# A four-layer graph and attention network on one core: residual sums, clamps, division and stores rearranged, with 20 unread matmuls on TensorE

## The reference, cut to what matters

```
x = x + y @ wo.T                                  # y: attention, softmax over keys, 4 heads
flat  = rmsnorm(x, ln2_w)
probs = softmax(flat @ router_w.T); tp, ti = top_k(probs, 2); tp = tp / (sum(tp) + 1e-9)
for e in range(8):
    hh  = silu(flat @ w1[e].T) * (flat @ w3[e].T)  # 341 hidden units
    out = out + weights[:, e] * (hh @ w2[e].T)
return x + out
```

## Time and profile before

| what | value |
|---|---|
| median of 3 runs | 590.49 us (589.0 to 591.74) |
| the profiled execution, its own time | 591.75 us |
| its span, first to last instruction | 590.0 us, mean granted clock 0.928 |
| TensorE busy | 493.3 us (84%) |
| VectorE busy | 435.3 us (74%) |
| ScalarE busy | 319.3 us (54%) |
| GpSimd busy | 265.2 us (45%) |
| DMA | 91.66 MB, mean 155 GB/s |

### The profile page before, as it was taken

One profiled execution on the slowest core, in us unless ns is written; L12 is line 12 of the kernel. 1 busy time (PEld: TensorE's weight loads), 2 busy tenths in 40 slices (PEclk: granted clock), 3 DMA queues, 4 the chain that ended last, 5 costly groups with the idle time before them and its releaser, 6 DMA issues.

```text
span 590.0 us, 11473 instructions
## 1 busy us (share of the span) xinstructions
PE 493.3 (84%) x3865; PEld 279.4 (47%) x3865; DVE 435.3 (74%) x1075; ACT 319.3 (54%) x533; POOL 265.2 (45%) x289
## 2 busy tenths in 40 slices
PE   2999994879999799998676788899899967878870
PEld 1534333567777645553332243232353246778860
DVE  6898947788999955647779498699977217848854
ACT  0787886867999500111143454476367626656750
POOL 3000003423455320200426589599827644868872
PEclk9999996999999989999868878999999968989995
DMA  8999973200008660011204341000112753869975
GB/s 302 398 423 422 420 257 107 90 20 16 24 18 347 253 143 14 0 41 40 70 3 134 106 127 50 30 2 1 65 49 74 248 189 95 269 215 388 339 261 162
DMA packets 39570, 91.66 MB, mean 155 GB/s; under 512 B 7488, under 2 KB 24944, under 8 KB 35168
## 3 DMA queue, kind: packets, MB, share of 16 engines
q1 hardware_dynamic: 35792, 86.11, 41.7%
q0 software_dynamic: 2272, 4.69, 2.2%
q10 hardware_dynamic: 1456, 0.22, 0.2%
HBM read 69.39 MB, written 19.23 MB: 150 GB/s over the span
## 4 chain that ended last, share of the span: by engine, by line
PE 57%; DVE 19%; issue 6%; DMA 6%; ACT 5%; POOL 4%; SPq 2%; DVEq 0%; ACTq 0%; POOLq 0%
PE ps L1375 9%; PE ps L1549 9%; DVE A L2347 7%; PE ps L1727 7%; PE ps L1460 6%; PE ps L1477 6%; PE ps L1719 3%; PE ps L1627 3%; POOL slots_in L1020 2%; PE ps L1574 2%; DMA A<-slots_out 2%; PE ps L1830 2%; PE ps L1352 1%; DVE bst L1878 1%; DMA slots_in<-R,A 1%
## 5 line engine op out<-in xcount | busy, mean ns | idle before, releaser
L2347 DVE TENSOR_REDUCE A<-ps 128x1 f32<-128x512 f32 (+3 forms) x160 | 86.4, 602 | 14.1 <-PE ps L1627 13.4
L1281 ACT ACTIVATE A<-ps 128x1024 f32<-128x1024 f32 (+3 forms) x80 | 68.5, 893 | 42.1 <-PE ps L1719 41.9
L975 POOL TENSOR_TENSOR G<-G,A 128x1024 f32<-128x1024 f32 (+3 forms) x40 | 73.9, 1876 | 9.3 <-ACT A L1281 9.1
L1627 PE MATMUL ps<-A 96*128 96x512 f16 (+3 forms) x160 | 55.2, 387 | 10.5 <-DVE A L2347 5.8
L1549 PE MATMUL ps<-A,G 128*128 128x512 f32 x128 | 62.0, 612 | 0.0
L1375 PE MATMUL ps<-R,G 128*128 128x512 f32 x128 | 59.2, 605 | 0.9 <-DVE G L1921 0.8
L1477 PE MATMUL ps<-R 128*128 128x128 f16 x768 | 48.2, 219 | 6.9 <-DVE x L2039 5.8
L1477 PEld LDWEIGHTS ps<-R 128*128 128x128 f16 x768 | 45.3, 98 | 14.4 <-issue 6.6
L2021 DVE SCALAR_TENSOR_TENSOR R<-R 128x512 f16<-128x512 f32 x64 | 46.8, 753 | 5.1 <-ACT R L1136 4.8
L1830 PE MATMUL ps<-A 128*128 128x128 f16 (+1 forms) x702 | 48.6, 227 | 1.7 <-DMA A<-w_split 1.7
L1134 ACT ACTIVATE R<-ps,b 128x512 f32<-128x512 f32 x64 | 44.0, 688 | 10.4 <-PE ps L1460 9.4
(11 more groups left out here) (309 smaller groups left out, 968.9 us busy)
## 6 DMA issues: line engine op xcount, KB each, us to landing
A<-w_split SPq DMA_DIRECT2D x39, 533.0 KB, 5.8
A<-in_adj_t SPq DMA_DIRECT2D x16, 1024.0 KB, 12.8
slots_in<-xn SPq DMA_DIRECT2D x1, 8320.0 KB, 22.4
R<-in_adj_in SPq DMA_DIRECT2D x7, 1024.0 KB, 5.4
xn<-in_adj_in SPq DMA_DIRECT2D x5, 1024.0 KB
w_split<-A SPq DMA_DIRECT2D x9, 533.0 KB, 3.3
xT<-in_adj_in SPq DMA_DIRECT2D x4, 1024.0 KB
A<-in_f_w SPq DMA_DIRECT2D x16, 170.5 KB
```

Source lines behind the costliest of these rows:

```text
L975: pool.tensor_tensor(total, total, probabilities(n, pair)[:, :, t0:CW], ALU.add).then_inc(s_sum, 1)
L1281: act.activation(probabilities(n, pair)[:, :, t0:CW], ps[:, 2 * pair:2 * pair + 2, t0:CW], ACT.Exp, scale=1.0 / (SQ * SQ * float(HD) ** 0. ...
L1627: last = pe.matmul(ps[:, bank, 0:width], queries(t // TPC, h)[0:KQ, P * (t % TPC):P * (t % TPC) + P], keys(b, h // (NH // NKV))[0:KQ, 0:wi ...
L2347: dve.reduce_max(pm[:, h, t % TPC, b:b + 1], ps[:, bank, 0:width], AX_X).then_inc(s_rmf, 1)
```

## The change

- **Residual sums.** GpSimd adds chunks 0 to 2 right behind its 24th scatter of rows, ahead of the root of the last chunk, and the last chunk behind `low_hidden(1)`; none is left between the scatters of outputs.
- **Clamps.** The targets of all slots of one row load (batches of 1, 3, 4, 4, 4, 4 and 2 slots) are clamped in one instruction at the batch's first slot: 7 instead of 22. The slots' homes in SBUF are shared out anew, so that no batch lies in two.
- **Division.** "db" is made of 4 transposes instead of 4 products by the identity, in all chunks. `o` of the last chunk is copied by VectorE, beside ScalarE's copy of `d`. ScalarE sums the squares ahead of slot 0's high half, VectorE makes the mean ahead of its low half.
- **Unread matmuls.** `spend(n)` issues n products of 128x128 by 128x512 in f16 into bank 3, which nothing reads: 5 ahead of "dt", 4 of "db", 4 of "out", 4 of slot 0's transpose, 2 of slot 0's hidden products and 1 of slot 1's.
- **Stores.** The stores of chunks 0 to 2 and of the last chunk's tiles 1 and 3 are issued by ScalarE, behind its last copy; SP issues those of tiles 0 and 2. The three loads of pairs have a semaphore each.

```diff
@@ homes of the slots
-        HOMES = [(15, G_flat), (7, A[:, 4, 2 * CW:]), (7, A[:, 5, 2 * CW:]), (10, R[:, ROWS_AT:])]
+        HOMES = [(15, G_flat), (6, A[:, 4, 2 * CW:]), (4, A[:, 5, 2 * CW:]), (14, R[:, ROWS_AT:])]
@@ semaphores
-        s_wst, s_pair = s_x[0:2], [s_x[2], *s_ld0, s_x[3], s_attw]
+        s_pairs = [s_x[2], s_row[2], s_x[0]]
+        s_wst, s_pair = s_x[0:2], [None, *s_ld0, s_x[3], s_attw]
@@ sync
-            for c in range(NC - 1):
-                store(c)
             sp.wait_ge(s_scat[1], 16 * (SLOTS - OPEN_END))
             for q in range(TPC):
                 load_pairs_of_tile(q)
-            for q in range(TPC):
-                store_tile(q)
+            for q in range(0, TPC, 2):
+                sp.wait_ge(s_fin, NC + q)
+                sp.dma_start(out[:, TPC * (NC - 1) + q, :], x[:, TPC * (NC - 1) + q, :]).then_inc(s_out, 16)
@@ gpsimd
             scatter_group(1)
+            for g in range(NC - 1):
+                residual(g)
             router_root(NC - 1)
...
             for n in range(LOW_IN_FRONT):
                 low_hidden(n)
+                if n == 1:
+                    residual(NC - 1)
...
                 scatter_output(n)
-                if n % 4 == 0 and n // 4 <= NC:
-                    residual(n // 4 - 1)
@@ scalar
-                    act.activation(o_sb[c], ps[:, 6, :], ACT.Copy).then_inc(s_od, 1)
+                    last = act.activation(d_sb[c], ps[:, 7, :], ACT.Copy)
+                    if c < NC - 1:
+                        last = act.activation(o_sb[c], ps[:, 6, :], ACT.Copy)
+                    last.then_inc(s_od, 1)
...
+            row_squares()
             slot_high(0)
-            row_squares()
...
+            for c in range(NC - 1):
+                act.wait_ge(s_fin, c + 1)
+                act.dma_start(out[:, TPC * c:TPC * c + TPC, :], x[:, TPC * c:TPC * c + TPC, :]).then_inc(s_out, 16)
+            for q in range(1, TPC, 2):
+                act.wait_ge(s_fin, NC + q)
+                act.dma_start(out[:, TPC * (NC - 1) + q, :], x[:, TPC * (NC - 1) + q, :]).then_inc(s_out, 16)
@@ tensor
-                        last = pe.matmul(ps[:, bank, P * q:P * q + P], inverse_rows[:, P * q:P * q + P],
-                                         ident[:, :], start=True, stop=True)
+                        last = pe.transpose(ps[:, bank, P * q:P * q + P], inverse_rows[:, P * q:P * q + P], ident[:, :])
...
+            def spend(count):
+
+                for _ in range(count):
+                    pe.matmul(ps[:, 3, :], ident_h[:, :], th[:, 0:CW], start=True, stop=True)
+
-            for what in ("dt", "db", "out"):
+            for what, count in (("dt", 5), ("db", 4), ("out", 4)):
+                spend(count)
                 unit((what, NC - 1))
+            spend(4)
             slot_transpose(0)
...
+                if k < 2:
+                    spend(2 - k)
@@ vector
-                if n >= FIRST:
-                    dve.tensor_tensor(target[:, n:n + 1], loaded_target(n), spare[:, n:n + 1], ALU.min)
+                count = BATCHES[batch_of[n]]
+                if n >= FIRST and n == ENDS[batch_of[n]] - count:
+                    dve.tensor_tensor(target[:, n:n + count], loaded_targets(n, count), spare[:, n:n + count], ALU.min)
...
-                dve.wait_ge(s_pair[0], AGAIN + 16 * (NC - 1))
+                dve.wait_ge(s_pairs[c], pairs_base[c] + 16)
...
+            dve.wait_ge(s_pv, len(steps))
+            chain(dve.tensor_copy(o_sb[NC - 1], ps[:, 6, :]))
             for what in ("dt", "db", "out"):
                 unit((what, NC - 1))
+            mean_square(NC - 1)
             slot_low(0)
-            mean_square(NC - 1)
```

More of the change, by code:

```diff
@@ L261, in program @@
         G_flat = G[:, :, :].rearrange("p t d -> p (t d)")
-        HOMES = [(15, G_flat), (7, A[:, 4, 2 * CW:]), (7, A[:, 5, 2 * CW:]), (10, R[:, ROWS_AT:])]
+        HOMES = [(15, G_flat), (6, A[:, 4, 2 * CW:]), (4, A[:, 5, 2 * CW:]), (14, R[:, ROWS_AT:])]
         homes = [home[:, RW * n:RW * n + RW] for count, home in HOMES for n in range(count)]
-        assert len(homes) == SLOTS and ROWS_AT + 10 * RW <= 4 * T
+        assert len(homes) == SLOTS and ROWS_AT + HOMES[-1][0] * RW <= 4 * T
         XB = 6
@@ L275, in loaded_target, with loaded_targets @@
             return slot_rows(n)[:, D + 1:D + 2].bitcast(I32)
+        def loaded_targets(n, count):
+            first = 0
+            for size, home in HOMES:
+                if first <= n < first + size:
+                    assert n + count <= first + size
+                    rows = home[:, RW * (n - first):RW * (n - first + count)].rearrange("p (s w) -> p s w", w=RW)
+                    return rows[:, :, D + 1].bitcast(I32)
+                first += size
         silu_sb = [A[:, 6 + n, 3 * CW:3 * CW + 3 * P] for n in range(2)]
@@ L467, in program @@
         s_scat = [sem(f"outputs_scattered_{w}") for w in ("early", "late")]
-        s_wst, s_pair = s_x[0:2], [s_x[2], *s_ld0, s_x[3], s_attw]
+        s_pairs = [s_x[2], s_row[2], s_x[0]]
+        pairs_base = [AGAIN, 16 * sum(row_buffer(i) == 2 for i in range(NT)), AGAIN + 16 * (E1 // 2)]
+        s_wst, s_pair = s_x[0:2], [None, *s_ld0, s_x[3], s_attw]
         steps = [(c, j) for c in range(NC) for j in [*range(TPC * c + TPC - 1, TPC * c - 1, -1), *range(TPC * c)]]
@@ L788, in load_pairs @@
                 sp.dma_start(pair_rows(c).rearrange("p (t w) -> p t w", t=TPC),
-                             src.rearrange("(t p n) d -> p t (n d)", t=TPC, n=2)).then_inc(s_pair[0], 16)
+                             src.rearrange("(t p n) d -> p t (n d)", t=TPC, n=2)).then_inc(s_pairs[c], 16)
             def load_pairs_of_tile(q):
@@ L795, in load_pairs_of_tile @@
                              slots_out[2 * P * t:2 * P * (t + 1), :].rearrange("(p n) d -> p (n d)", n=2)).then_inc(s_pair[1 + q], 16)
-            def store(c):
-                sp.wait_ge(s_fin, c + 1)
-                sp.dma_start(out[:, TPC * c:TPC * c + TPC, :], x[:, TPC * c:TPC * c + TPC, :]).then_inc(s_out, 16)
-            def store_tile(q):
-                t = TPC * (NC - 1) + q
-                sp.wait_ge(s_fin, NC + q)
-                sp.dma_start(out[:, t, :], x[:, t, :]).then_inc(s_out, 16)
             for b in range(4):
@@ L1305, in _ @@
                     act.wait_ge(s_pv, n + 1)
-                    act.activation(d_sb[c], ps[:, 7, :], ACT.Copy)
-                    act.activation(o_sb[c], ps[:, 6, :], ACT.Copy).then_inc(s_od, 1)
+                    last = act.activation(d_sb[c], ps[:, 7, :], ACT.Copy)
+                    if c < NC - 1:
+                        last = act.activation(o_sb[c], ps[:, 6, :], ACT.Copy)
+                    last.then_inc(s_od, 1)
             def silu(n):
```

## The result

The changed kernel took 583.57 us (median of 4 executions, 581.97 to 585.54) against 591.06 (589.0 to 591.74) for the kernel before on the same chip: ratio 0.9881, interval 0.984 to 0.9921. So it is faster, by 4.7 to 7.0 us by the three ratios, 5.8 by their mean (0.9901 of 590.5). Each of these ratios is uncertain by 2 us or so.

A forecast was written before the change was run, and what follows sets the result against it. It took chains of waits as the bound: the closing relay through SP, the last division, and the slots with DMA full. Terms 0.4 + 0.7 - 0.6 + 0.3 + 0.2 + 1.6 + 0.8 = 3.4 us, from 590.49 to 587.1, range 584.2 to 590.6.

The forecast's parts named there:

- its own signs of being wrong: Last scatter no earlier than 578, L1830 of the first two slots both near 2.1, or an end below 584.
- Division in chunks 0 to 2: In attention, transposes replace the products of "db": bounds 0 and 1.2 us, taken as 0.4 gained.
- Last division: Behind chunk 3: sum ready at about 481.4 instead of 484.04, but slot 0 still waits until 484.17; no gain, no cost.
- Slots 0 and 1: First slots' products under the clock with unread products: bounds -0.9 and +1.9 us, taken as +0.7.
- The middle case: In the first two slots: clock falls in the hole, slot 0 runs at half, clock rises behind it; +0.9 us.
- Fourth residual: Last chunk's residual starts where the router's small steps run and delays the late scatters: bounds 0 and -1.1 us, taken as -0.6.
- Late slots: Residuals no longer meet clamps, 15 clamps go, but DMA is full: bounds -0.8 and +2.6 us, taken as +0.3.
- the argument from the full DMA: In the later slots DMA share is 1.03 from 540 to 553, so time gained turns into waits for weights.
- grown waits for weights: Sign of being right: waits of L1830 for w_split grown; no size given.
- Tail: End of the kernel: last scatter +0.2 us, SP no longer behind the stores +1.6, last loads sharing DMA with no chunk stores +0.8.
- The relay's 1.6: At the end, SP issued the last pair loads 1.6 us late, behind the third store; moving stores gains +1.6.
- separate semaphores nothing: At the end, one semaphore per pair load gains nothing, since VectorE is later than all three loads.

The follow-up runs named there:

- e3_again: The changed kernel without its 20 unread products: ratio 0.9897 against the kernel before (0.9901 when the same edit ran on another chip).
- e7: The kernel before with the residual sums alone moved: ratio 0.9958 against the kernel before.
- e10: The kernel before with the stores on other queues and the residual sums moved, clamps and homes as before: ratio 0.9977.
- after: First profile of the changed kernel, nothing else changed: the profiled execution took 583.83 us, span 582.1.
- after 2: Further profile of the changed kernel, nothing else changed: ratio 0.9903 against the kernel before.
- e9: The changed kernel with the fourth residual ahead of the router and 14 instead of 4 unread products ahead of slot 0: 584.25 us, ratio 0.9875.
- e1: The kernel before with "db" made of transposes in all four chunks, nothing else changed: ratio 0.991, on a slower chip.
- after_again: The changed kernel itself, run again as a control on a slower chip: ratio 0.992 against the kernel before.
- e12: The changed kernel with the additions of chunks 0 to 2 waiting for all three pair loads again: ratio 0.9931 against the kernel before.

## Why the prediction was wrong, point by point

The sign was right; the sum was 3.4, the ratios give 4.7 to 7.0, the two profiles 7.9. Two terms were too small, the division in chunks 0 to 2 (0.4, measured 1.05 or more) and the late slots (0.3, measured 0.75 with a wide spread). Two steps failed in their mechanism: that nothing could use the router's earlier root (it gave some 1.2 us), and that the pairs of chunks 0 to 2 would be loaded before VectorE is free. That the terms of the tail add up to the measured sum all the same is in part luck. Of its own signs of being wrong one came: an end below 584 (582.1).

- **Division in chunks 0 to 2:** the term that was mis-sized. I took 0.4 of a bound of 1.2: all of it for chunk 2's "db", none for those of chunks 0 and 1, because VectorE's row maxima hold TensorE there. Chunk 2's "db", which lies in chunk 3, gave 0.50, nearly the whole difference of 0.53. But the other two, in chunks 1 and 2, gave 0.22 and 0.33: VectorE hid half of it, not all. Together 1.05, and 1.28 where the low stretch of the clock falls into chunk 1.
- **Last division:** right in its times, wrong in what it gives. It took 3.10 busy of 3.50 us at full clock, the sum was ready 6.10 us behind the last step's end (forecast 6.09, 8.73 before), and slot 0 waited for its rows all the same (8.80 and 9.08 us from the last step, 8.86 and 8.71 before). But the step that put it at nothing failed: "TensorE could not use it sooner, since slot 0's products stand before 'tr'". Before, TensorE waited 0.87 and 0.65 us between these products and "tr", for rows that hang on the root. In the seven undisturbed profiles with the old division "tr" starts 4.33 or 4.34 us behind the first row transpose, in `e3_again` 3.36, and 3.88 to 4.19 with the unread products.
- **Slots 0 and 1:** size about right, cause wrong. The middle case (half in slot 0, full in slot 1) happened to the letter and brought slot 1's products forward by 0.64 us (from 5.43 to 4.79 behind the first row transpose; 0.7 was taken), but without the unread products it is 1.0 (4.43). The step that failed compared the slots' own durations and left out that the products are paid for where they stand. What did shorten this stretch is in the rest of the division's edits: 21.15 with the fourth residual but the old division (`e7`, `e10`), 19.81 to 20.19 with the new, so 1.2 us. In `e3_again` 1.07 of it is there by the start of the logits (6.28 instead of 7.35 us behind the first row transpose). The edits of the last division were not tried one by one.
- **Fourth residual:** -0.6 forecast, -0.9 measured by the stretch, -1.0 by taking it out; within its bounds, by the mechanism named.
- **Late slots:** +0.3 forecast, 1.9 in the first profiles. Over the five profiles with both edits (68.10, 68.20, 68.53, 69.90, 70.37) and the four with neither (70.0, 70.29, 69.50, 69.29) the means are 69.02 and 69.77: +0.75, where single executions spread by 2. The first two profiles of the changed kernel were the two shortest. The clamps alone gave nothing. What became of TensorE's waits, counted from 20 us behind the first late scatter: those for VectorE, 2.2 to 3.4 us in the five undisturbed profiles with the residuals of before (mean 2.7), are gone in all seven with moved ones, and those for row and weight loads rose from a mean of 5.4 to one of 7.3. Of 2.7 gained 1.9 went into waits for DMA, and 0.8 is left. So the argument from the full DMA held. The sign that was named, grown waits for weights, did not come in the first profile (1.7 before, 0.8 after); on the means they grew, from 0.6 to 1.3.
- **Tail:** +2.6 forecast for scatter, relay and sharing. Relay and end together went from a mean of 12.36 to one of 9.60 over four profiles (after, after 2, `e3`, `e9`): +2.8; the last scatter -0.1 instead of +0.2 (3.69 on the mean of those four, 3.59 before). The relay's 1.6 is what both pairs of profiles give, but as the sum of two things that were not forecast: the queues alone give 2.2, and the early additions, which hold the last scatters, take part of it back. On the slower chips the tail gave less, 9.90 in `e1` (tail of before) against 8.79 in `after_again`. And one step was wrong: "separate semaphores nothing, since VectorE is later than all three loads". The forecast had output 31's scatter 4 to 5 us earlier against the end of the slots because four residuals are gone, so 13 to 15 us ahead of the last scatter. It was 9.67 ahead, and 9.84 before. Already in the kernel before, GpSimd had caught up with the outputs behind its last residual (its scatter at 549.96 is released by ScalarE's copy), so these 5.1 us did not hold output 31. The pair loads came later than VectorE, which was free at 567.4 (1.73 before 569.12) and waited for the first load alone; with one semaphore for all three the stores meet the last loads, and the end is 8.19 to 8.52 long, longer than before, instead of 0.8 shorter.
- **What was no part of any term:** of the 7.9 us between the first profiles, 0.5 lie at the start, where the code is the same (282.50 to 285.16 over all kernels), and 1.9 in chunks 0 and 1, where the second profile of the kernel before had a like gain over its first (91.73 against 93.65).

By stretches the schedule gives 1.05 + 0.3 + 0.75 + 2.65 = 4.75 us (0.3 is 20.25 less 19.98, the mean of after, after 2, `e3` and `e12`; 2.65 is relay and end less the last scatter). That is the low end of the ratios, and inside the interval of each. The microsecond beside their mean of 5.8 is open, or 1.6 us beside the 6.4 of the two ratios from undisturbed chips. One candidate: chunks 0 and 1 together took over 93 us in 8 of 10 profiles with products and in 4 of 10 with transposes, the means being 93.26 and 92.18. If that is no chance, the transposes also make the low clock rarer there, and give 1.9 in place of 1.05; ten profiles each don't settle it. As for the range, the late slots alone vary by 2 us from one execution to the next, and the low end of 584.2 left little room for terms that err on the same side.

## What to carry to other kernels

Ask of each shared semaphore which waiter could start on the first of several transfers; what it does earlier may move another transfer out of the way of the last one. A store moved to another queue removes the wait in front of what stood behind it, not its bytes: look at what it then runs beside. And before a stage's gain is explained, take a second profile of the unchanged kernel: here it moved chunk 1 by 1.4 us. And before an earlier result is priced at nothing, look in the trace for the wait of the engine that takes it.

## What the runs showed of the hardware

On the two slower chips the kernel before takes 616.35 and 613.03 us. There chunk 3 takes 61.4 to 65.2 us instead of 49.1 to 49.6 and the late slots 79.9 to 84.2 instead of 68.1 to 72.2, and ScalarE, VectorE, GpSimd and TensorE each stand still for 1 to 4 us at a time with no releaser that the trace shows. One such place in the changed kernel:

```profile
447.04 0.26 ACT L1257 ACTIVATE R<-R 128x64 f32<-128x64 f32 x1 [2.44 <-issue]
450.58 1.94 ACT L1285 ACTIVATE A<-ps 128x1024 f32<-128x1024 f32 x2 [3.28 <-remote]
```

In the other measurements, the first among them, it is absent. What it is was not found; it begins where GpSimd's row scatters do, which is a coincidence in time and no more. With it one execution differs from the next by up to 8 us (604.25 to 611.9 for the changed kernel), so ratios there say less.

A mark that hardly moves: in the 12 profiles without these standstills slot 0's first row transpose comes 8.70 to 9.08 us behind the end of the last attention step, with either division, at either clock, with 0 to 30 unread products. Its rows arrive by GpSimd's scatters, which follow the steps; so a mark like this is good for comparing stages, and no work on TensorE in front of it shows.
